# Two shared units moved to the end, gather slots made chunk by chunk, and pair weights fetched with one unchecked load

## The reference

```
gates  = softmax(h @ router_w)                 # 14 experts
top 2 experts e1, e2 with weights, normalised to sum 1
routed = w_e1 * ffn_e1(h) + w_e2 * ffn_e2(h)   # ffn: rms norm, silu(h @ W1) @ W2, 128 -> 256 -> 128
shared = ffn_s0(h) + ffn_s1(h)                 # two experts that every token takes
out    = x + routed + shared
```

## Time and profile before

| | |
|---|---|
| median of three runs | 327.97 us |
| the profiled execution | 328.76 us |
| its span in the trace | 327.0 us |
| TensorE, matmuls | 261.0 us busy, 80% of the span |
| VectorE | 227.5 us busy, 70% |
| GpSimd | 163.1 us busy, 50% |
| ScalarE | 163.0 us busy, 50% |
| gather DMAs on GpSimd (L651) | 64, 65.4 us busy |

### The profile page before, as it was taken

How to read it: one execution, slowest core, us unless ns; L and a number is a source line. 1 busy time by engine, 2 the same in 40 slices (tenths; PEclk the granted TensorE clock), 3 DMA queues, 4 the chain that set the end, 5 groups by cost and what they waited for, 6 DMA issues and landing times.

```text
span 327.0 us, 8789 instructions
## 1 busy us (share of the span) xinstructions
PE 261.0 (80%) x2812; PEld 236.7 (72%) x2812; DVE 227.5 (70%) x818; ACT 163.0 (50%) x318; POOL 163.1 (50%) x218
## 2 busy tenths in 40 slices
PE   1794664884498689999998799898979999999920
PEld 0794553774376467888887699897979999998920
DVE  6999998589932488678778744868546767765432
ACT  1477645469676465666655634243434444443300
POOL 2589200000074006777777777300556777777771
PEclk9999587599599996999999899999999999999985
DMA  5693028968999911111111254322454656664431
GB/s 142 177 386 131 0 68 228 248 180 239 323 309 323 295 46 34 48 52 56 51 48 55 77 160 141 98 74 87 139 154 112 192 166 185 188 170 139 119 82 48
DMA packets 72725, 47.17 MB, mean 144 GB/s; under 512 B 6240, under 2 KB 70128, under 8 KB 72176
## 3 DMA queue, kind: packets, MB, share of 16 engines
q1 hardware_dynamic: 66000, 37.07, 38.7%
q0 software_dynamic: 4096, 8.40, 8.7%
q10 hardware_dynamic: 2592, 1.26, 1.5%
HBM read 28.66 MB, written 18.06 MB: 143 GB/s over the span
## 4 chain that ended last, share of the span: by engine, by line
PE 37%; DVE 25%; issue 16%; POOL 11%; ACT 3%; DVEq 3%; DMA 3%; POOLq 1%; SPq 0%; ACTq 0%
POOL area L651 11%; PE bank L1606 5%; PE bank L1593 4%; PE bank L1690 3%; PE bank L1433 3%; PE bank L1701 3%; PE bank L1495 2%; PE bank L1533 2%; PE bank L1541 2%; PE bank L1534 2%; PE bank L1422 2%; DVE stats L703 2%; DVE st L813 2%; DVE u L748 2%; DVE area L808 2%
## 5 line engine op out<-in xcount | busy, mean ns | idle before, releaser
L651 POOL DMA_INDIRECT area<-y_dram,u x64 | 65.4, 1022 | 46.9 <-DMA y_dram<-u 28.9
L632 POOL DMA_INDIRECT xs_dram<-area x64 | 63.8, 996 | 41.9 <-issue 40.3
L1005 DVE COPY v<-v 128x512 f32 x84 | 35.9, 436 | 20.4 <-issue 19.9
L1690 PE MATMUL bank<-xn,v 128*128 128x128 f32 x320 | 43.7, 279 | 1.2 <-DVE v L1005 0.9
L1690 PEld LDWEIGHTS bank<-xn,v 128*128 128x128 f32 x320 | 38.8, 191 | 3.7 <-issue 1.3
L1701 PE MATMUL bank<-v,xn 128*128 128x128 f32 x312 | 41.2, 275 | 0.0
L1701 PEld LDWEIGHTS bank<-v,xn 128*128 128x128 f32 x312 | 38.0, 192 | 0.0
L1358 ACT ACTIVATE xn<-bank 128x512 f32<-128x512 f32 x40 | 23.9, 598 | 22.7 <-PE bank L1690 22.7
L1353 ACT COPY xn<-bank 128x256 f32<-128x256 f32 x41 | 15.2, 371 | 29.0 <-PE bank L1681 29.0
L1090 DVE SCALAR_TENSOR_TENSOR x_sb<-area,u,x_sb 128x128 f32<-128x128 f32 x64 | 18.4, 349 | 11.8 <-DMA area<-y_dram,u 10.7
L1068 DVE COPY u<-bank 128x256 f32<-128x256 f32 x39 | 16.3, 418 | 12.2 <-PE bank L1701 11.3
(11 more groups left out here) (318 smaller groups left out, 605.9 us busy)
## 6 DMA issues: line engine op xcount, KB each, us to landing
area<-kp_dram SPq DMA_DIRECT2D x12, 512.0 KB, 6.1
y_dram<-xinit SPq DMA_DIRECT2D x1, 4992.0 KB, 19.1
area<-xs_dram SPq DMA_DIRECT2D x78, 64.0 KB
y_dram<-u SPq DMA_DIRECT2D x39, 128.0 KB
x_sb<-in_L_attn_x SPq DMA_DIRECT2D x4, 512.0 KB, 8.5
area<-ab_dram SPq DMA_DIRECT2D x2, 1024.0 KB, 6.4
xn<-ab_dram SPq DMA_DIRECT2D x2, 1024.0 KB, 11.4
xn<-kp_dram SPq DMA_DIRECT2D x4, 512.0 KB, 6.9
```

The source lines that it names most:

```text
L632: pool.indirect_dma_start(out=xs_dram.ap(), out_offset=bass.IndirectOffsetOnAxis(ap=pos[:, k, i:i + 1], axis=0), in_=hx[:, i, :], in_offse ...
L651: pool.indirect_dma_start(out=yl[:, k, i, :], out_offset=None, in_=y_dram.ap(), in_offset=bass.IndirectOffsetOnAxis(ap=slot_of[:, k, i:i + ...
L1005: v.tensor_copy(wc[:, z % STEP], v1_flat.rearrange("p (w m) -> p w m", w=2)[:, :, bass.ds(r, HID)]).then_inc(wc_ready, 1)
L1690: last = mm(bank[2 + p % 2][:, HID * j + P * c:HID * j + P * c + P], wc[:, (2 * p + j) % STEP, 1, P * c:P * c + P], xsT[:, p % 3, P * j:P ...
```

## The change

- `fetch_weights` loads both offsets of a pair with one register load and without the bounds check; the first four places of the ring are filled from one load of four.
- `block_steps` stands ahead of the end of pair 0 and not behind it. The slots are made chunk by chunk: after pairs 4c to 4c+3, VectorE compares, weighs, sums and finishes chunk c for both routes, each on 128 x 224 elements (224 = 2 x 4 x 28), and counts `slot_ready` up by one. GpSimd waits for `slot_ready` of its chunk.
- `ltab` has 24 entries: for each chunk and each of the three semaphores the exact count. By the blocks above the pairs to wait for become 7, 13, 15, 20, 23, 28, 31 and 36.
- `results_in` is one semaphore for each chunk and route, and not one for each chunk.
- The two units of the fill are gone from it; eight units stand behind the loop (`SH_FIRST, SH_FILL, SH_LOOP, SH_TAIL` = 18, 0, 1, 8).

```diff
-    SH_FIRST, SH_FILL, SH_LOOP, SH_TAIL = 18, 2, 1, 6
+    SH_FIRST, SH_FILL, SH_LOOP, SH_TAIL = 18, 0, 1, 8
...
-        last_of = area[:, 12888:12888 + CH]
+        last_of = area[:, 12888:12888 + CH * ROUND]
...
-            pool.wait_ge(slot_ready, 1)
             for c in range(CH):
+                pool.wait_ge(slot_ready, c + 1)
                 for z in range(ROUND):
-                    pool.wait_ge(y_out[z], landed[c])
+                    pool.wait_ge(y_out[z], landed[ROUND * c + z])
                     g_.sem_inc(pool_turn, 1)
                 for k in range(2):
                     for i in range(TILES * c, TILES * c + TILES):
                         pool.indirect_dma_start(out=yl[:, k, i, :], out_offset=None, in_=y_dram.ap(),
...
-                                                bounds_check=NBLK * P - 1, oob_is_err=False).then_inc(results_in[c], 16)
+                                                bounds_check=NBLK * P - 1, oob_is_err=False).then_inc(results_in[c][k], 16)
...
-            v.tensor_scalar(last_of[0:1], size_to[0:1, E - 1:NGRP:E], 1.0 / (2 * ROUND),
+            v.tensor_tensor(last_of[0:1].rearrange("p (c z) -> p c z", c=CH),
+                            size_to[0:1, E - 1:NGRP:E].unsqueeze(2).broadcast_to([1, CH, ROUND]),
+                            iota_e[0:1, 0:2 * ROUND:2].unsqueeze(1).broadcast_to([1, CH, ROUND]), ALU.subtract)
+            v.drain()
+            v.engine_nop().then_inc(btab_ready, 1)
+            v.tensor_scalar(last_of[0:1], last_of[0:1], 1.0 / (2 * ROUND),
                             (2 * ROUND - 1) / (2 * ROUND) - 0.5 + 1.0 / (4 * ROUND), ALU.mult, ALU.add)
             v.drain()
-            v.engine_nop().then_inc(btab_ready, 1)
...
-            def fetch_weights(at, z):
-                r = dve.value_load(etab[0:1, bass.ds(at, 1)], min_val=0, max_val=(E - 1) * HID)
-                v.tensor_copy(wc[:, z % STEP], v1_flat.rearrange("p (w m) -> p w m", w=2)[:, :, bass.ds(r, HID)]).then_inc(wc_ready, 1)
+            def fetch_weights(at, n=2):
+
+                _, rows = nc.values_load_multi_w_load_instructions(
+                    etab[0:1, at:at + n], engines=[mybir.EngineType.DVE], min_val=0, max_val=(E - 1) * HID,
+                    skip_runtime_bounds_check_because="an entry counts the experts whose blocks have ended, E - 1 at most")
+                for z, r in enumerate(rows, at):
+                    v.tensor_copy(wc[:, z % STEP], v1_flat.rearrange("p (w m) -> p w m", w=2)[:, :, bass.ds(r, HID)]).then_inc(wc_ready, 1)
...
-            def pass_bounds(k):
+            def pass_bounds(c):
+                v.tensor_tensor(passed, pos[:, :, TILES * c:TILES * c + TILES].unsqueeze(3).broadcast_to([P, 2, TILES, 2 * E]),
+                                tiles_by(bounds[:, c]), ALU.is_ge)
...
-                if k == 0:
-                    dve.wait_ge(results_in[c], 16 * 2 * TILES)
+                dve.wait_ge(results_in[c][k], 16 * TILES)
...
+            block_steps()
+            v.drain()
             summed = 0
             for q in range(PAIRS):
                 if q >= ROUND:
                     dve.wait_ge(y_out[q % ROUND], 16 * (q // ROUND))
                 finish_pair(q, q % STEP)
-                if q == 0:
-                    block_steps()
...
+                if q < 4 * CH:
+                    if q % 4 == 0:
+                        pass_bounds(q // 4)
+                    elif q % 4 == 1:
+                        weigh_bounds(q // 4)
+                    elif q % 4 == 2:
+                        sum_bounds(q // 4)
+                    else:
+                        finish_slots(q // 4)
...
-            add_tail(SH_LAST, 4)
-            for n in range(2 * (CH - 2), 2 * (CH - 1)):
-                add_results(n // 2, n % 2)
-            add_tail(SH_LAST + 4, SH_TAIL - 4)
-            for n in range(2 * (CH - 1), 2 * CH):
-                add_results(n // 2, n % 2)
+            for u_ in range(SH_LAST, NT, 4):
+                add_tail(u_, min(4, NT - u_))
+                for c in range(u_ // 4, min(u_ + 4, NT) // 4):
+                    add_results(c, 0)
+                    add_results(c, 1)
...
-                if p >= 1:
-                    if p >= 2:
-                        pe.wait_ge(so_added, SH_FIRST + p - 1)
-                    shared_out_loop(SH_FIRST + p - 1, p - 1)
-                if p < SH_FILL:
-                    shared_in_loop(SH_FIRST + p)
```

More of the change, by code:

```diff
@@ L368, in build_kernel @@
         slot_ready = sem("slot_ready")
-        results_in = [sem(f"results_in{c}") for c in range(CH)]
+        results_in = [[sem(f"results_in{c}_{k}") for k in range(2)] for c in range(CH)]
         sum_ready = sem("sum_ready")
@@ L376, in tail_out @@
         def tail_out(u_):
-            return (7, 0)[(u_ - SH_LAST) // 4]
+            return (7, 0)[(u_ - SH_LAST) // 4 % 2]
         def in_bank(u_):
@@ L510, in _ @@
                         sp.nop().then_inc(xs_in[z], 16)
-                if stored < CH and q >= PAIRS_TO[stored] + 8:
+                if stored < SH_LAST // 4 and q >= PAIRS_TO[stored] + 8:
                     store(stored)
@@ L1068, in finish_pair @@
                 v.tensor_copy(yb[:, z:z + 2], bank[4 + p % 2][:, 0:2 * D].rearrange("p (j d) -> p j d", j=2)).then_inc(yb_ready, 2)
-                for j in range(2):
-                    fetch_weights(q * 2 + (STEP + j), z + j)
+                fetch_weights(q * 2 + STEP)
             def share_gates():
@@ L1372, in _ @@
                     silu(it * (UNROLL // 2) + (STEP // 2 + p + 1), STEP // 2 + p + 1)
-                    if p == 0:
+                    if SH_LOOP and p == 0:
                         act.wait_ge(so_ps, it * SH_LOOP + SH_BASE)
@@ L1739, in tail_unit_out @@
                 pe.wait_ge(sh_ready, u_ + 1)
+                if u_ >= SH_LAST + 8 and (u_ - SH_LAST) % 4 == 0:
+                    pe.wait_ge(so_added, u_ - 4)
                 at = P * ((u_ - SH_LAST) % 4)
```

50 lines of the change are left out of this document (18 added, 32 removed).

## The result

Four runs of the changed kernel took 316.9 to 318.51 us, a median of 317.73 us; four of the kernel before beside them 325.57 to 328.4 us, a median of 327.74. The ratio is 0.971, with a 95% interval of 0.967 to 0.975: faster by 10 us. The profiled execution took 317.75 us, its span is 316.0 us. The forecast was 317 us. Ratios here go by executions in the chip's fast state alone; the highest time of experiment 8, 330.31 us, is of a slow one.

A forecast was written before the change was run, and what follows sets the result against it. GpSimd's gather chain, started by chunk 1's store, was taken to bound the kernel: 235.8 + 72.85 + 6.66 = 315.3 us, equal to TensorE's chain; with 1.76 outside the span, 317 us, range 313 to 323.

The forecast's parts named there:

- Fill: TensorE's start of the stage: three bare pairs at 2.01 us take 6.03 us against 11.15, so the loop starts 5.1 earlier.
- the two covers that the prediction named: VectorE in the fill: 3.44 us idle ahead of pair 0 hides `block_steps`; a 0.4 us slots piece fits under TensorE's 2.01.
- Fetching weights: VectorE's weight copies: about half of 17.3 us idle ahead of them goes; charged nothing in the loop, where VectorE waits for TensorE.
- Loop: TensorE's loop: 90.80 us less 2.0 for VectorE's gather waits gives 88.8; the 1.89 us stall at 240.75 stays in.
- Exact waits: GpSimd's first gathers: chunk 0 at about 222.6 us, chunk 1 at 235.8 instead of 246.34; no wait for later chunks.
- Steps of the gather: GpSimd's gathers from chunk 1 on: 55 steps stay at 1.325 us each, 72.85 us; copies affect a gather at most 0.22.
- third rival: Back-to-back VectorE copies hold GpSimd's gathers by up to 0.43 us each, steps of 1.755 us, 341 us; chance 0.05.
- Behind the last gather: End of the gather chain: four additions instead of eight, then the store; 2.60 + 1.2 + 2.86 = 6.66 us.
- Tail: TensorE's eight units behind the loop at 1.85 us end at 309.4; additions and store bring its chain to 315.3 us.
- the first: Row loads hold bare pairs in the fill and first pass, losing 3.7 of the 5.1 us gained: 321 us; chance 0.22.
- The second: More comes free: first pass sheds small waits, chunk 1 no longer waits for a store, 314.5 us; chance 0.15.
- The fourth: Counts stay rounds in effect, or gather starts late for registers or slots: 322.5 us, or 326 with fill's gain lost; chance 0.06.

The follow-up runs named there:

- experiment 8: Kernel before with only the new weight fetch (one unchecked register load for a pair's two copies): median 325.37 us, ratio 0.999.
- its repetition: The changed kernel itself, unaltered, run and profiled again beside a version with three things more: median 319.79 us, ratio to the kernel before 0.976.
- experiment 1: Changed kernel with the two units back in the fill and six behind the loop: median 323.0 us, ratio to the kernel before 0.9865.
- experiment 5: Changed kernel with `block_steps` behind the end of pair 0 again: one run, 319.7 us.
- experiment 3: Changed kernel with slots made in two halves for all chunks, pieces on 128 x 896 elements after pairs 1 to 6: median 317.46 us, ratio 0.975.
- experiment 4: Changed kernel with the old fetch, one checked register load for each block's weights: median 318.66 us, ratio 0.977.
- experiment 2: Changed kernel with the counts of stored pairs rounded up to whole rounds again: median 322.04 us, ratio 0.985.
- experiment 9: Changed kernel without the weight copies and their register loads in the pairs: one run, 315.97 us.
- experiment 6: Changed kernel without the four additions of the last chunk's second route: one run, 316.13 us.
- experiment 7: Changed kernel with row loads behind even pairs, one pair earlier: one run, 319.16 us.
- experiment 11: Changed kernel plus no units in the loop's first two passes, earlier row loads, GpSimd's register entries in two halves: medians 314.22 and, repeated, 316.45 us.
- the last version: The kernel of experiment 11; its repetition had a median of 316.45 us, ratio to the kernel before 0.9675.

## Why the prediction was right, step by step

**The forecast's mechanism held; two terms of its sum were too small, and an early start of the profiled execution hid it.** From the first transposition to the span's end, the forecast's gather chain is 315.3 - 197.93 = 117.4 us; after shows 316.0 - 195.63 = 120.4, and its repetition 119.8. The 3.0 us are 1.68 of longer steps, 1.16 at the end and 0.15 at chunk 1's gather; the start gave back 2.30, and that is luck. The second median, 319.79 us, is 0.9% above the forecast, still in its range. The gain was overrated: 11.8 us from the profiled 328.76 us, against 10.0 between the medians of the first series and 7.6 in the second (327.4 to 319.79).

- **Fill.** Forecast 6.03, measured 6.01 us. Experiments 1 and 8 show the parts: the units 3.6, the shorter fetch 1.2 (11.15 to 9.98); the remaining 0.4 was not separated. Of the two covers that the prediction named, one was needed: without the idle time `block_steps` costs chunk 1's gather 2.1 us (experiment 5). The other was not. A piece of slots takes 0.38 us, forecast 0.4, but the prediction's price for a piece of 1.09 us, 2.67 us a pair and 2.0 us given back, is refuted by experiment 3, where pieces of that length left the fill at 6.02 us and chunk 1 at 38.0.
- **Fetching weights.** Charged at nothing in the loop, because VectorE waits for TensorE there. That failed: with the old fetch the changed kernel's loop takes 4.2 us more (experiment 4).
- **Loop.** Forecast 88.8, measured 87.89 us (87.5 in the repetition): near in size, but not by the parts forecast. Before's 90.80 us hold the stall of 1.89 us, which the forecast kept in as having no cause in the trace. It was a late row load. The transposition at 240.75 is pair 16's, which needs blocks 32 and 33, loaded behind store 11 from 236.20 on the earlier trace rows; by the trace's record of landings block 33's parts came by 238.73 but for one, at 240.66 (five of its sixteen are not recorded). Why that part came 1.9 us late stays open; no later profile has a wait for row loads of more than 0.9 us. Without it before's loop takes 88.9 us, so about 1.0 us is left for all else. The 2.0 us ascribed to gather waits are therefore not shown. With the new fetch in place, 89.94 falls to 87.89 as four waits of 6.3 us go (experiment 8 against after, which differ in more than that), but one wait of 1.35 us back in the loop costs nothing (experiment 2, 87.46); with the old fetch the loop is longer without any such wait, 92.05 us (experiment 4, which also has the slots' pieces in the loop). That either delay of VectorE hides the other's removal is a reading of these four, not shown by a run of its own.
- **Slots.** Nothing, as forecast (experiment 3).
- **Register load.** 24 steps and a load of 2.0 us lie within the bounds, but the load began later against the stage (210.9 - 195.63 = 15.3 us behind the first transposition, before 12.0), so GpSimd was ready at 218.4, 1.2 us ahead of its first gather: hidden, with less in hand than forecast.
- **Exact waits.** Chunk 0's first gather at 24.7 us by the forecast, 23.9 measured; chunk 1's at 37.9 and 38.0. Experiment 2 gives the counts alone 3.7 us there, experiment 1 the units 2.7, experiment 5 `block_steps` 2.1, experiment 4 the fetch 1.1: 9.5 us in sum against 10.4 from before to after. This is not a full account, for each is the loss of one part with the others in place. And the stall of before stands ahead of pair 14's second matrix, so it held store 14 too: VectorE copied the result at 243.22 and the store went out at 243.68, while the loads ahead of it in the queue had ended at 240.50 + 1.93 = 242.43. Up to 1.2 of the 10.4 us are this stall's and not the change's; the forecast, which started from store 12, did not rest on it. No wait behind chunk 1, as forecast.
- **Steps of the gather.** Forecast 1.325, measured 1.355 us: 74.53 - 72.85 = 1.68 us, and the repetition has 1.355 again. This is the first term that was mis-sized, and its cause is the third rival's mechanism in small: with copies one after the other the mean gather goes from 1.022 to 1.048 us, without copies it is 1.009 (experiment 9); experiments 4 and 8 lie between before and after, at 1.028 and 1.040. A gather that meets copies takes 0.06 us more on the mean, not the rest of a copy. Single ones take more: the prediction's bound of 0.22 us did not hold for the longest, 1429 ns against a shortest of 992. The Trainium skill, page "SBUF — State Buffer", section "SBUF: two separate sides", has GpSimd's descriptor writing blocked while VectorE copies float32 in its two-port mode. The trace agrees in direction: the copies do lengthen gathers, by hundredths of a microsecond; the rule's full hold at every such gather, and the 341 us of that rival, did not occur.
- **Behind the last gather.** Forecast 6.66, measured 7.82 us. This is the second mis-sized term: the prediction took the additions and the store for what stands last, but GpSimd's DRAIN ends the span 7.8 us behind the start of the last gather, whatever VectorE does there (experiment 6). Making the second route's additions four instead of eight brought nothing.
- **Tail.** Forecast 14.8, measured 14.65 us. TensorE's chain would have ended at 306.93 + 2.35 + 2.86 = 312.1, 116.5 behind the first transposition against a forecast of 117.4.

Of the rivals, the first was there in part, by one of the prediction's own signs of being wrong: TensorE's wait of 0.87 us for row loads in the first pass, and 2.5 us at chunk 1's gather that came free when the loads moved (experiment 7), less than the 3.7 us it was priced at. The second did not come about: chunk 1 still waits for a store, 3.64 us after and 2.48 us even in experiment 11, which reaches that rival's time by other means. The fourth is excluded by experiment 2. Its place in the prediction's bookkeeping was a slip: counted as within 1%, it was priced with rounds alone at 322.5 us, 1.9% under the profiled time and inside the range that was said to leave it out.

## What to carry to other kernels

Read a stage by distances from its own first instruction: here the work ahead of it moved profiled spans by up to 5 us, more than most single changes were worth. When several engines finish together at the end of a trace, the tail behind the last work has more than one possible owner, and shortening one of them is worth nothing until the others are ruled out. A delay of zero for an edit on an engine that "waits anyway" holds only while the other waits of that engine stay: price it again for the state that the rest of the change leaves. And a stall that the profile names no releaser for can be a transfer that came late once: before a forecast keeps it, or an experiment is credited with its absence, look up when the transfers that the instruction needs landed.

## What the runs showed of the hardware

GpSimd's closing DRAIN ended 7.6 to 7.7 us behind the start of the last gather in all fourteen profiles, and the span 7.8 to 8.0 us behind it in thirteen of them, with eight, four or no additions in between; in the other, experiment 4, the last store came later (8.1 us). The gather's DMA itself had been seen by VectorE 2.6 us behind its start (308.18 to 310.80).

One register load of 24 entries on GpSimd took 1997 ns, one of 8 entries 773 ns, two of 12 entries in the repetition of the last version 822 and 1015 ns: each less than in proportion to the load of 8.
